# A graph network on one core: streams of four-edge chunks, and finished sums scattered by GpSimd before the next gather

## What is computed

```
fs = x @ Ws + bs; fd = x @ Wd + bd                      # gatv2, twice
e = leaky_relu(fs[src] + fd[dst], 0.2)
logits = einsum('ehd,hd->eh', e, attn)
m = segment_max(logits, dst); ex = exp(logits - m[dst])
alpha = ex / segment_sum(ex, dst)[dst]
out = elu(segment_sum(alpha * fs[src], dst))            # then a layer norm
# then, on the sum with x, normed again:
mean = segment_sum(x[src], edge_type * n + dst) / max(cnt, 1)
h1 = einsum('rni,rio->no', mean, W_rel) + x @ W_root + b_rgcn
xw = h1 @ W_gcn                                         # all in f32
out = segment_sum(xw[src] * norm, dst) + xw * dinv**2 + b_gcn
```

## Time and profile before

| | before |
|---|---|
| median of 3 runs | 3333.24 us |
| the profiled execution, first to last instruction | 3343.9 us |
| PE busy | 2854.4 us, 85% |
| DVE busy | 2290.3 us, 68% |
| ACT busy | 1702.4 us, 51% |
| POOL busy | 1620.6 us, 48% |
| granted TensorE clock, mean | 0.947 of full |

### The profile page before, as it was taken

The page is one execution under the profiler, slowest core; times in us unless marked ns, Lnnn a source line. Parts: engine busy times, 40 slices in busy tenths (PEclk is TensorE's granted clock), DMA queues, the critical chain, the costliest instruction groups (busy, mean ns, idle before and its releaser), DMA issues. The chain is left out here.

```text
span 3343.9 us, 59649 instructions
## 1 busy us (share of the span) xinstructions
PE 2854.4 (85%) x13556; PEld 2139.5 (64%) x13557; DVE 2290.3 (68%) x4351; ACT 1702.4 (51%) x5372; POOL 1620.6 (48%) x2067
## 2 busy tenths in 40 slices
PE   5885888888789799998668999999999976777799
PEld 3442454454455455554348999999999974555598
DVE  6535889889767788887565555555555447888743
ACT  0004889899722133332545566555665566777300
POOL 4666566565446555554114545544544445555201
PEclk9897999999999899999789999999999998999899
DMA  4235344444511555555228777777776747666412
GB/s 141 84 81 159 121 135 126 124 134 124 170 46 44 157 167 170 171 170 175 89 95 263 243 242 245 242 237 237 247 241 219 222 144 230 203 210 208 119 34 65
DMA packets 175008, 546.00 MB, mean 163 GB/s; under 512 B 55331, under 2 KB 56343, under 8 KB 174723
## 3 DMA queue, kind: packets, MB, share of 16 engines
q0 software_dynamic: 82000, 370.33, 35.3%
q1 hardware_dynamic: 70596, 122.50, 11.8%
q10 hardware_dynamic: 22304, 52.11, 5.4%
HBM read 461.31 MB, written 83.81 MB: 163 GB/s over the span
## 5 line engine op out<-in xcount | busy, mean ns | idle before, releaser
L2189 PE MATMUL pO<-wh,gT 128*128 128x384 f32 x3264 | 867.1, 339 | 17.6 <-ACT gT L2140 15.6
L805 POOL DMA_INDIRECT row<-fs_d,rec x400 | 455.9, 1140 | 389.6 <-PE pA L1330 157.5
L2189 PEld LDWEIGHTS pO<-wh,gT 128*128 128x128 f32 x3264 | 594.4, 189 | 26.4 <-ACT gT L2140 23.0
L2189 PE MATMUL pO<-wl,gT 128*128 128x384 f32 x1632 | 547.5, 335 | 0.0
L2203 DVE TENSOR_SCALAR cntge<-pT 128x768 int32<-128x768 int32 x137 | 131.2, 958 | 427.2 <-ACT gT L2140 223.1
L1038 ACT ACTIVATE sj<-sj 128x96 f32<-128x96 f32 x1176 | 312.9, 268 | 78.7 <-DVE sj L1155 78.5
L2189 PEld LDWEIGHTS pO<-wl,gT 128*128 128x128 f32 x1632 | 308.3, 189 | 0.0
L2140 ACT ACTIVATE gT<-cntge 128x256 fp32r<-128x256 f32 x822 | 292.9, 410 | 28.1 <-DVE cntge L2206 4.0
L805 POOL DMA_INDIRECT row<-y_d,rec x200 | 204.1, 1020 | 171.6 <-PE pR L2335 113.5
L1077 PE MATMUL pS<-row,ident 128*128 128x384 f32 x400 | 176.2, 524 | 128.3 <-DVE sj L1155 80.9
L2335 PE MATMUL pR<-row,share 128*128 128x384 f32 x384 | 165.7, 582 | 120.6 <-issue 65.0
(11 more groups left out here) (386 smaller groups left out, 5983.8 us busy)
## 6 DMA issues: line engine op xcount, KB each, us to landing
fdt<-in_L_gnn_W_rel_dram SPq DMA_DIRECT2D x170, 384.0 KB
startrow<-seen_d ACTq DMA_DIRECT2D x141, 320.0 KB
raw<-in_L_gnn_W_rel_dram SPq DMA_DIRECT2D x34, 384.0 KB
row<-fs_d,rec POOLq DMA_INDIRECT x400
kept_d<-fdt SPq DMA_DIRECT2D x10, 384.0 KB
kept<-kept_d SPq DMA_DIRECT2D x10, 384.0 KB
fs_d<-of SPq DMA_DIRECT2D x9, 388.0 KB
fd_d<-of SPq DMA_DIRECT2D x9, 388.0 KB
```

Source lines behind the costliest of these rows:

```text
L805: pool.indirect_dma_start(b["row"][u][:, j, :].bitcast(words), None, table, bass.IndirectOffsetOnAxis(ap=b["rec"][u][:, 2 * j + field:2 * ...
L2189: last = pe.matmul(pO[:, q, 0:HALF], gT[:, c, half, :].bitcast(F32R), w[:, c, lo:up].bitcast(F32R), start=c == 0 and k == 0, stop=c == KC ...
```

## The change

The tiles are gone as the unit of the stream. Each partition now has a stream of its own: the nodes that it was given, ten of them, one from each tile with the order within every other tile turned round, lie behind one another chunk by chunk, and group g takes the g-th chunk of every partition. So a group can end one node in one partition and be in the middle of another in the next. A table of 16 words per chunk and partition (`info`) says the record's row, the node, whether the chunk is the node's first, and where its sum goes when it is the last (`R_OUT`; past the end of the table where it isn't, and such rows aren't written). The number of groups is that of the partition with most chunks, rounded up to turns of four.

The running sum goes from one group's buffer to the next (`total`, four buffers). After each group POOL sends the buffer's finished rows to a table in device memory by one indirect DMA (`sums_out`): `first_d`, `second_d`, `ysum_d`. The rows of `fd` are no longer held on chip by tile; one more indirect DMA per group gathers them (`own_of`), in both attentions. In step u POOL now waits for the signals of group u-1 that its sum is complete (`done`), sends that sum, and then fetches the rows of group u+2.

The settling stages read their input in the nodes' order by plain DMAs. `settle_last` computes a weight for each edge on POOL (`weigh`), 48 groups in 8 parts. The edge counts of stage (h) are made by 192 indirect DMAs that add into a table in device memory (`tally`), three per pair in the first 64 pairs of the relation products; they have gone from stage (g), and so have the weights. The weights' table has a loop of its own for groups beyond 48; as written it makes at least one turn, with four such adding DMAs. Stage (h) loads its counts from that table, and writes the output by plain DMAs.

```diff
+                    v.link(dve.tensor_tensor_scan(chunk_end[:], chunks[:], chunks[:], 0.0, ALU.add, ALU.max))
+                    dve.sem_inc(ends_ready, 1)
+                    v.link(dve.tensor_tensor(chunk_from[:], chunk_end[:], chunks[:], ALU.subtract))
+                    v.mark(dve.tensor_tensor(of_chunk[:, 0, :], byrank[:, :, 2], chunk_from[:], ALU.subtract))
+                    v.mark(dve.scalar_tensor_tensor(out=of_chunk[:, 1, :], in0=chunk_from[:], scalar=float(S), in1=degree,
+                                                    op0=ALU.mult, op1=ALU.add))
...
+                        w.mark(dve.scalar_tensor_tensor(out=word(R_OUT), in0=is_last, scalar=float(NP), in1=node,
                                                         op0=ALU.mult, op1=ALU.add))
...
+        def keep_target(pool, b, i, off):
+            u = off % U
+            sum_free(pool, b, i, off)
+            n = off // U + 1 + (u == U - 1)
+            pool.sem_inc(b["posted"], 1)
+            pool.tensor_copy(b["to"][u][:], word(b, u, R_OUT)).then_inc(b["to_ok"][u], 1)
+            pool.wait_ge(b["to_ok"][u], i + n)
+            pool.sem_inc(b["posted"], 1)
+        def sums_out(pool, b, off, table):
+            u = off % U
+            pool.indirect_dma_start(table, bass.IndirectOffsetOnAxis(ap=b["to"][u][:], axis=0), b["sum"][u][:], None,
+                                    bounds_check=NP - 1, oob_is_err=False).then_inc(b["sum_out"][u], 16)
...
+            def fetch(i, off):
+                u = off % U
+                pool.wait_ge(b["edges_only"][(u - 1) % U], i * 16 + 16 * ((off - 1) // U + 1))
+                rec_wait(pool, b, i, off)
+                pool.sem_inc(b["posted"], 1)
+                pool.tensor_scalar(edge[:], slot[:].rearrange("p s c -> p (s c)"), word(b, u, R_LEFT, F32), None, ALU.is_lt)\
+                    .then_inc(b["edge_ok"], 1)
+                pool.wait_ge(b["edge_ok"], i * U + (off + 1))
+                pool.sem_inc(b["posted"], 1)
+                edges_only(u)
+                keep_target(pool, b, i, off)
+                pool.wait_ge(b["edges_only"][u], i * 16 + 16 * (off // U + 1))
+                pool.sem_inc(b["posted"], 1)
+                used.wait(pool, i, off - U)
+                pool.sem_inc(b["posted"], 1)
+                rows_of(pool, b, u, table, 0, F32)
+                own_of(pool, b, u, own)
...
-                    w = u + ROWS_AHEAD
-                    pool.wait_ge(b["rec_in"][w % U], i * 16 + 16 * (w // U + 1))
+                    record(w % U)
+                    for s in done:
+                        s.wait(pool, i, u - 1)
                     pool.sem_inc(b["posted"], 1)
-                    v.wait()
-                    edges_only(w % U)
-                    pool.wait_ge(b["edges_only"][w % U], i * 16 + 16 * (w // U + 1))
-                    pool.sem_inc(b["posted"], 1)
-                    used.wait(pool, i, w - U)
-                    pool.sem_inc(b["posted"], 1)
-                    rows_of(pool, b, w % U, table, 0, F32)
-                    assert v.n == PER * (u + 1), (v.n, PER)
-            pool.wait_ge(b["rec_in"][U - 2], turns * 16 + 16)
+                    sums_out(pool, b, u - 1, out_table)
+                    fetch(i, u + ROWS_AHEAD)
...
+        def gather_rows(pool, b, table, field, own, out_table, readers, done, words=F32):
+            open_sums(pool, b)
+            def fetch(i, off):
+                u = off % U
+                rec_wait(pool, b, i, off)
+                pool.sem_inc(b["posted"], 1)
+                keep_target(pool, b, i, off)
+                for used in readers:
+                    used.wait(pool, i, off - U)
+                pool.sem_inc(b["posted"], 1)
+                if own is not None:
+                    own_of(pool, b, u, own)
                 rows_of(pool, b, u, table, field, words)
...
             with pool.Fori(0, turns) as i:
                 for u in range(U):
-                    w = u + ROWS_AHEAD
-                    pool.wait_ge(b["rec_in"][w % U], i * 16 + 16 * (w // U + 1))
-                    for used in readers:
-                        used.wait(pool, i, w - U)
+                    for s in done:
+                        s.wait(pool, i, u - 1)
                     pool.sem_inc(b["posted"], 1)
-                    rows_of(pool, b, w % U, table, field, words)
+                    sums_out(pool, b, u - 1, out_table)
+                    fetch(i, u + ROWS_AHEAD)
...
-                        gather_edges(pool, b, fs_d[0:1 + N], summed, others)
+                        gather_edges(pool, b, fs_d[0:1 + N], fd_table, first_d, summed, (added, den_ok))
...
-                        def finish(i, off, tile):
+                        def finish(i, off):
                             summed.wait(dve, i, off)
                             scaled_ok.wait(dve, i, off)
-                            dve.tensor_tensor(split(acc[:, ds(tile, 1), :].rearrange("p o f -> p (o f)")), halves(pA),
-                                              split(scaled[:]), ALU.add).then_inc(added.sem, 1)
-                        def arguments(v, i, u, tile):
+                            sum_free(dve, b, i, off)
+                            dve.tensor_tensor(split(total[off % U][:, 0:D]), halves(pA), split(scaled[:]), ALU.add)\
+                               .then_inc(added.sem, 1)
...
-                        gather_rows(pool, b, fs_d[0:1 + N], 0, (summed,))
+                        gather_rows(pool, b, fs_d[0:1 + N], 0, fd_d, second_d, (summed,), (kept, den_ok, counted))
...
+                        def keep(i, off):
+                            whole.wait(act, i, off)
+                            sum_free(act, b, i, off)
+                            act.activation(split(total[off % U][:, 0:D]), halves(pA[off % 2]), ACT.Copy).then_inc(kept.sem, 1)
...
+                        def weigh(v, groups, weight):
+                            ge, rel = cge[:, 0:groups], crel[:, 0:groups]
+                            of_node = crow[:, 0:groups, :].unsqueeze(2).to_broadcast([P, groups, S, RELS])
+                            v.link(pool.tensor_tensor(rel, ge[:, :, :, 0:RELS], ge[:, :, :, 1:RELS + 1], ALU.subtract))
+                            v.link(pool.tensor_tensor(rel, rel, of_node, ALU.mult))
+                            n = RELS
+                            while n > 2:
+                                half = n // 2
+                                v.link(pool.tensor_tensor(rel[:, :, :, 0:half], rel[:, :, :, 0:half], rel[:, :, :, n - half:n], ALU.add))
+                                n -= half
+                            v.link(pool.tensor_tensor(weight, rel[:, :, :, 0], rel[:, :, :, 1], ALU.add))
...
+                        for part in range(EARLY // PART):
+                            at = part * PART
+                            pool.dma_start(cge[:].rearrange("p g s r -> p g (s r)"), ge_d[:, 1 + at:1 + at + PART, :]).then_inc(cge_in, 16)
+                            for g in range(PART):
+                                pool.indirect_dma_start(crow[:, g, :], None, rcnt_d, bass.IndirectOffsetOnAxis(
+                                    ap=crec[:, at + g, R_NODE:R_NODE + 1], axis=0)).then_inc(crow_in, 16)
+                            pool.wait_ge(crow_in, 16 * (at + PART))
+                            pool.wait_ge(cge_in, 16 * (part + 1))
+                            weigh(v, PART, cweight[:, at:at + PART, :])
...
+                    def tally(out, j):
+                        pool.wait_ge(counted, out * (16 * PER_PAIR) + 16 * j)
+                        pool.sem_inc(posted, 1)
+                        pool.indirect_dma_start(counts_d, bass.IndirectOffsetOnAxis(ap=cindex[:, j:j + 1], axis=0),
+                                                ones[:, 0:1], None, compute_op=ALU.add).then_inc(counted, 16)
+                    def pair(v, i, n, out, counting=False):
+                        if counting:
+                            pool.wait_ge(counted, out * (16 * PER_PAIR))
+                            pool.sem_inc(posted, 1)
+                            v.link(pool.tensor_copy(cindex[:], cells[:, ds(out * PER_PAIR, PER_PAIR)]))
                         for b in range(PAIR):
                             make_list(v, i, n, b + PAIR)
+                            if counting:
+                                tally(out, 2 * b)
                             t_ok.wait(pool, n, b)
                             pool.sem_inc(posted, 1)
                             fetch(b)
                             if out is not None:
                                 put(v, out, n, b - PAIR)
+                            if counting and b == 0:
+                                tally(out, 1)
...
+                        pair(v, i + 1, i * PAIR + PAIR, i, True)
...
-                    gather_rows(pool, b, y_d, 1, (used, summed), words=I32)
+                    gather_rows(pool, b, y_d, 1, None, ysum_d, (used, summed), (used,), I32)
```

1129 lines of the change are left out of this document (572 added, 557 removed).

## The result

The changed kernel takes 5065.2 us, the median of 4 runs (5056.0 to 5074.3), against 3332.4 us for the kernel before (4 runs, 3331.2 to 3335.2): a ratio of 1.520, 95% interval 1.517 to 1.523. The prediction was 4880 us, in a range of 4530 to 5200. The profiled execution spans 5054.5 us, 1710.6 more than before's, where the sum had +1545.

A forecast was written before the change was run, and what follows sets the result against it. Engines bound the old attention loops; the added wait was to close a loop through one group. Terms 609 + 676 - 38 + 43 + 240 + 15 = +1545 on 3343.9 give 4889, less 10.7 for the median: 4880 us, range 4530 to 5200.

The forecast's parts named there:

- The gate and the loop: Both attentions: POOL's wait for group u-1's sum before fetching u+2 closes a loop through one group; +609 and +676 us.
- The other signs: Attentions: PE's first pass released by a gather at half rate, granted clock well below 0.9, DVE and ACT under half busy.
- The rival in which the clock does not come back: Attentions: PE stays at 1.2 GHz through its burst, loops 35.4 and 32.2 us, 5510 us in all; chance 8%.
- Its terms: First attention, per group: hand-over 0.3, write 1.0, small operations 1.9, gathers 10.3, PE 13.0, DVE's sum and hand-over 1.05 us.
- The half rate: Attentions: after idling for the rows PE starts each group at the 1.2 GHz level, costing 2.6 us a group.
- The low-clock rule: Attentions: a loop waiting longer for DMA than it computes can drop the clock every round; 229 us in all.
- Third pass and the rest: Third pass over the edges: POOL-bound at 7.3 us a group, -38 us; projections, first settling and last products together +15.
- its tail: `settle_last`, behind the eight weight parts: stored weights and one turn of the later-groups loop with four adding DMAs, 31 us.
- 5.7 - 1.9 = 3.8 us a pair: Relation products: three adding DMAs, a copy and a landing wait, less POOL's slack, over 64 pairs; +240 us.
- The slack: Relation products: of POOL's 2.30 us wait in a pair, 1.9 us could take added work without cost.
- The sign "POOL has no wait left": Relation products: POOL becomes the bound and has no wait left in the first 64 pairs.

## Why the prediction came out as it did

**The gate and the loop.** Right in mechanism and in sum. The first attention's loop was forecast at 27.6 us and is 28.48, the second's at 25.6 and is 25.39. Three runs show the mechanism itself: the pace halves when the gate moves behind the fetch, when TensorE's order changes (second attention), and when both TensorE's and VectorE's do (first). One thing the prediction had wrong here: it named TensorE's order as what closes the loop. In the first attention VectorE's order closes it a second time; TensorE's alone gave back only 2.7 us. The other signs came too: in both attentions every one of the 44 first passes is released by a gather and at half rate, the granted clock is 0.72 and 0.70, and VectorE and ScalarE are busy under half of the time. The rival in which the clock does not come back is out: the passes are at 0.81 us again 3.7 us after the first.

**Its terms** partly cancel, and that the sums come within 3% is in part luck. In the group shown the way back to POOL took 0.96 us (0.3 taken), the write with the small operations 3.66 (2.9), the gathers 9.70 (10.3), TensorE 12.25 (13.0). The write was 1.67 us, not 1.0: no row of before had shown rows past the bound, but the cost was not in skipping them, since the second attention's writes skip too and take 1.01 (the last section has what goes with it). The half rate was taken for 2.6 us a group and is worth 1.9; its stretch was 3.7 us long, not 5.2. The mean round is 0.95 us longer than the one shown, for which the sum had no term.

**The low-clock rule** of the Trainium skill that the prediction cited ("TensorE: Matmul & The Clock Gate", section "HAM oscillation — how this bites in real kernels") says the drop comes with each round of such a loop. The trace agrees: all 44 first passes behind the wait are at half rate in each attention, and the run with 23 more matmuls gave 83 us of the first back.

**Third pass and the rest.** -27 for -38, and 7.55 us a group for 7.3: POOL is full, as forecast, with no idle time of over 1.4 us in its loop. All else came to -3 for +15; the table of chunks is hidden.

**`settle_last`**, +78 for +43, was mis-sized at its tail: 62 us behind the parts for 31, and 31 ahead of them for 25. The eight parts are 18.6 us apart on the mean (18.9 forecast), which is partly luck: the first took 16.7 us, with 6.5 for the elementwise work that was forecast at 7.8, and in later ones the same instructions are longer (up to 20.7 us a part). Behind them POOL's timeline has:

```profile
3087.60 2.33 POOL L1910 DMA_DIRECT2D groups_d<-cweight  x1 [0.30 <-POOL cweight L1877]
3102.87 0.57 POOL L1921 DMA_DIRECT2D crec<-groups_d  x1 [12.93 <-issue]
...
3114.39 1.68 POOL L1935 DMA_INDIRECT counts_d<-ones,ccell  x1 [0.30 <-issue]
3120.82 1.58 POOL L1935 DMA_INDIRECT counts_d<-ones,ccell  x1 [4.75 <-DMA counts_d<-ones,ccell]
3126.59 1.55 POOL L1935 DMA_INDIRECT counts_d<-ones,ccell  x1 [4.19 <-DMA counts_d<-ones,ccell]
```

12.9 us before the loop's first load, for which I had no term of its own, and 6.1 us from one awaited adding DMA to the next, where a single gather's landing (3.2) had let me take 3.5. The four adding DMAs make 10 of the tail's 31 us too many. The 12.9 us are for the most part a landing: the program waits there until the stored weights are in device memory, and the DMA issues of this stretch have (KB, then us from issue to landing)

```profile
groups_d<-cweight POOLq DMA_DIRECT2D x1, 96.0 KB, 13.5
```

What the rest of the 31 is stays open, since the prediction gave the tail's terms only in part.

**Relation products**, +338 for +240: the term that was mis-sized is "5.7 - 1.9 = 3.8 us a pair"; it is 5.3 (338 by 64). The adding DMAs and the list of the next tile in the groups by line, the list of the kernel before first:

```profile
L2059 POOL TENSOR_SCALAR sourcef<-total 128x1 f32<-128x1 f32 x138 | 28.4, 206 | 217.5 <-ACT acc L2129 212.3 <-issue 2.9 <-DMA g<-hr_d,gindex 2.2
```
```profile
L2220 POOL TENSOR_SCALAR sourcef<-total 128x1 f32<-128x1 f32 x138 | 78.8, 571 | 67.3 <-ACT sign L2311 36.4 <-POOL cindex L2251 28.8 <-DMA g<-hr_d,gindex 2.0
L2243 POOL DMA_INDIRECT counts_d<-ones,cindex x192 | 319.7, 1665 | 248.4 <-DMA counts_d<-ones,cindex 142.9 <-POOL keys L2223 41.7 <-PE pT L169 31.3
```

The adding DMA takes 1.67 us on the mean, not the 1.26 of the small scatter: 1.2 us a pair more. The wait for its landing was taken at 0.5 us and is 2.2, of which 0.9 would be there anyway: 0.8 more. The slack was taken at 1.9, and 2.7 of the wait for ScalarE are gone (212.3 to 36.4): 0.8 less. That gives 5.0 of the 5.3. Some 40 us of the stage's 98 too many lie in the last eight of the 64 pairs, which took 22 to 27 us where the others mostly took 17 to 21; there the second and third DMA of a pair wait 2.0 to 5.5 us for a landing, and why they land so late is open. The sign "POOL has no wait left" came for ScalarE and not for these landings.

In the changed kernel POOL uses up its slack whole. That it isn't free wherever it is used shows only in the two runs with one adding DMA. And PE's busy time rose from 956 to 1072 us for the same 5718 passes, at a clock of 0.88: once PE waits at all, it also works at half rate in part of the stage. The prediction left that out here; whether it costs anything while POOL sets the pace is not shown.

## What to carry to other kernels

When an engine's queue waits for a result before it fetches, write down for every engine which later data stand ahead of that result in its own order; if one of them is what is fetched, the whole round trip is paid per step, and the sum of its parts gives its length (here within 3%, with errors that cancelled). Issue the fetch first, and send a result so late that neither it nor the landing of its buffer's last write is waited for, the index buffers counted too; two groups late with four buffers did it here. Slack on an engine is free only where nobody waits for what stands behind it: one DMA a pair cost 155 us ahead of a gather and 25 us behind the scatter.

## What the runs showed of the hardware that was not expected

**GpSimd's DMAs beside VectorE.** The same write took 1.02 or 1.67 us. In the run with both orders changed, two writes on POOL, and VectorE at the time of the second:

```profile
658.54 1.02 POOL L884 DMA_INDIRECT first_d<-sum,to  x1 [1.09 <-DVE sum L1254]
...
676.83 1.67 POOL L884 DMA_INDIRECT first_d<-sum,to  x1 [5.27 <-DVE sum L1254]
```
```profile
656.63 0.96 DVE L1254 TENSOR_TENSOR sum<-pA,scaled 128x768 f32<-128x768 f32 x1 [0.92 <-PE pA L1191]
659.83 1.83 DVE L1224 TENSOR_TENSOR sj<-row,own 128x768 f32<-128x768 f32 x2 [2.24 <-DMA own<-fd_d,rec]
...
675.80 1.82 DVE L1224 TENSOR_TENSOR sj<-row,own 128x768 f32<-128x768 f32 x2
```

VectorE is idle during the first, and adds two operands from on-chip memory during the second. It is so throughout: in this run VectorE worked beside all 23 long writes and beside one of the 22 short ones. In the changed kernel's first attention it worked beside the 44 long writes and not beside the one short one, and in the second attention 44 of the 45 writes took 1.01 or 1.02 us with VectorE idle, and beside the one of 1.35 us it worked. The Trainium skill, "SBUF — State Buffer", section "Who interferes with whom", says that a VectorE instruction with two SBUF inputs contends with a GpSimd instruction that reads SBUF. The rows agree with that, as far as they go: no run changed VectorE's work alone, so contention as the cause of the long writes is argued, and of the longer gathers in the relation products still more so.

**The half rate after short idle times.** With 20 matmuls in the wait, 2.4 us idle and more behind 13 us of full work were enough in 26 of 44 rounds. In the run with both orders changed 16 first passes behind 2.1 to 3.5 us of idle time took 0.91 us, and five behind 3.3 to 3.6 us took 1.64. The idle time alone doesn't decide.

**An adding DMA** of 128 single words holds POOL for 1.55 to 2.05 us (a gather of 128 whole rows 0.95), and where a small operation stands right behind it, that one is longer too, 0.8 us where 0.19 is usual.
